# Cross attention with the keys on the partitions, and its softmax run beside the next sequence's projections

## The reference

```python
q = (x @ Wq).reshape(B, N, 8, 64).transpose(0, 2, 1, 3)        # x: layer-normed, N = 128
k = (context @ Wk).reshape(B, M, 8, 64).transpose(0, 2, 1, 3)  # M = 2048
v = (context @ Wv).reshape(B, M, 8, 64).transpose(0, 2, 1, 3)
attn = softmax(einsum('bhnd,bhmd->bhnm', q, k) * scale, axis=-1)
out = einsum('bhnm,bhmd->bhnd', attn, v)
```

## Time and profile before

| | |
|---|---|
| median of 3 runs | 1711.84 us (1708.66 to 1711.86) |
| the profiled execution, own time | 1703.06 us |
| its span, first to last instruction | 1701.1 us |
| PE busy | 1634.1 us (96%) |
| DVE, ACT, POOL busy | 648.4, 663.5, 541.3 us (38%, 39%, 32%) |
| granted clock of PE | 0.99 on average |

### The profile page before, as it was taken

The page is one execution under the profiler, slowest core; times in us unless marked ns, Lnnn a source line. Parts: engine busy times, 40 slices in busy tenths (PEclk is TensorE's granted clock), DMA queues, the critical chain, the costliest instruction groups (busy, mean ns, idle before and its releaser), DMA issues. The chain is left out here.

```text
span 1701.1 us, 23083 instructions
## 1 busy us (share of the span) xinstructions
PE 1634.1 (96%) x9230; PEld 1290.6 (76%) x9231; DVE 648.4 (38%) x1079; ACT 663.5 (39%) x1196; POOL 541.3 (32%) x326
## 2 busy tenths in 40 slices
PE   7999999999999999999999999998889998999998
PEld 6667887887887888788788888773457686877876
DVE  6316325424523523632532542444365461222222
ACT  3225334434433533533433443342444433354421
POOL 6221132044043023124113304003620046768661
PEclk9999999999999999999999999999999998999999
DMA  5230121121111021021012112014200076656521
GB/s 209 88 99 26 39 68 50 32 74 50 32 63 46 17 81 50 26 73 59 25 32 75 50 32 81 1 36 170 75 1 1 21 259 143 172 148 188 162 56 35
DMA packets 70393, 125.15 MB, mean 74 GB/s; under 512 B 12000, under 2 KB 28448, under 8 KB 70304
## 3 DMA queue, kind: packets, MB, share of 16 engines
q1 hardware_dynamic: 40192, 92.14, 16.6%
q10 hardware_dynamic: 25296, 23.34, 4.7%
q0 software_dynamic: 4816, 8.41, 2.6%
HBM read 100.74 MB, written 24.43 MB: 74 GB/s over the span
## 5 line engine op out<-in xcount | busy, mean ns | idle before, releaser
L220 POOL TENSOR_TENSOR ctx_h<-stage,one 128x1024 fp32r<-128x1024 f32 x62 | 117.4, 1894 | 759.1 <-PE ps_t L288 759.1
L288 PE MATMUL ps_s<-ctx_h,wk 128*128 128x512 f32 x1024 | 325.4, 393 | 9.3 <-DVE ctx_l L498 9.3
L288 PE MATMUL ps_t<-wv,ctx_h 128*128 128x512 f32 x1024 | 317.7, 392 | 0.0
L542 DVE TENSOR_TENSOR kT<-ps_s,kT 64x512 fp32r<-64x512 f32 x128 | 87.5, 683 | 426.2 <-ACT kT L455 425.4
L288 PEld LDWEIGHTS ps_s<-ctx_h,wk 128*128 128x128 f32 x1024 | 193.5, 189 | 49.7 <-issue 9.9
L288 PEld LDWEIGHTS ps_t<-wv,ctx_h 128*128 128x128 f32 x1024 | 192.3, 188 | 42.3 <-issue 2.9
L564 DVE TENSOR_REDUCE smax<-ps_s 128x1 f32<-128x1024 f32 x128 | 150.6, 1218 | 142.1 <-PE ps_s L306 140.9
L288 PE MATMUL ps_s<-ctx_l,wk 128*128 128x512 f32 x512 | 200.3, 391 | 0.0
L288 PE MATMUL ps_t<-wv,ctx_l 128*128 128x512 f32 x512 | 199.3, 389 | 0.0
L438 ACT ACTIVATE probs<-ps_s,nmax 128x1024 f32<-128x1024 f32 x128 | 142.0, 1123 | 91.6 <-DVE nmax L567 91.6
L454 ACT ACTIVATE kT<-ps_s 64x512 fp32r<-64x512 f32 x128 | 75.6, 591 | 261.8 <-PE ps_s L288 168.3
(11 more groups left out here) (236 smaller groups left out, 2228.1 us busy)
## 6 DMA issues: line engine op xcount, KB each, us to landing
stage<-in_ctx_dram SPq DMA_DIRECT2D x64, 512.0 KB, 3.8
raw_u<-in_up_dram SPq DMA_DIRECT2D x32, 512.0 KB, 4.0
stage<-in_down_dram SPq DMA_DIRECT2D x16, 512.0 KB, 4.0
raw_e<-in_down_dram SPq DMA_DIRECT2D x16, 512.0 KB, 4.1
rows_scratch<-wxo SPq DMA_DIRECT2D x25, 256.0 KB, 4.6
wxo<-rows_scratch ACTq DMA_DIRECT2D x23, 256.0 KB, 3.4
q_scratch<-kT ACTq DMA_DIRECT2D x4, 1024.0 KB, 5.5
qa<-q_scratch ACTq DMA_DIRECT2D x32, 128.0 KB, 3.0
```

The costliest lines, as they stand in the source:

```text
L220: nc.gpsimd.tensor_tensor(hi, raw, one[:, 0:1].unsqueeze(2).broadcast_to([P, 2, QT]), ALU.mult).then_inc(hi_done, 1)
L288: mm = nc.tensor.matmul(out, w(c), m(c), start=(c + k == 0), stop=(c == DC - 1 and k == 2))
L542: nc.vector.tensor_tensor(kT[XD:P, 0, p, keys], ps_s[0:XD, p, :], kT[0:XD, 0, p, keys], ALU.subtract)
```

## The change

**What it does.** (1) Keys on the partitions: the weights of a score product are now 128 keys of one pair (`kT`, both heads' 64 dimensions on 128 partitions), and the moving side is `q2`, 256 columns: for head 0 its queries on the first 64 partitions and zeros on the others, for head 1 the other way (block diagonal). High and rest are again three products. Per group and pair there are 4 x 3 = 12 matmuls of 256 columns, 192 per sequence. The 128 transposes, their copies and the ACT accumulator go. (2) Scores are made group by group, and ACT copies them to `s` in SBUF (`copy_score`), DVE keeps a running maximum in `top` (`max_scores`), and `kT` holds one group only. (3) The largest score of a latent is now across partitions: PE turns the maxima (`turn_max`), DVE reduces them and puts them on a diagonal (`diagonal`), PE spreads them to all partitions by a product with ones (`spread_max`), DVE subtracts (`shift`, 128x2048 per head), ACT does exp (`exps`), POOL adds up the 16 chunks (`tree`), and PE sums over the partitions (`sums`). DVE takes the reciprocal of a 128x512 tile (`output`). (4) Shift, exp and tree of sequence b-1 run while PE projects sequence b; its `values` stand behind the value projections of b's first group. After the last sequence they have nothing beside them, and half of the row sums are made on PE (`sums_of_chunks`). (5) ACT makes `ctx_h` (`round_ctx`), POOL only the rest. (6) Sequence 0 begins with the values of two groups, and the key exit is one 128-partition instruction each on ACT and DVE.

```diff
-                        keys = kT[:, h % 2, h // 2, j * 512:(j + 1) * 512]
-                        nc.tensor.matmul(ps_s[:, j, :], qa[:, h, :], keys, start=True, stop=False)
-                        mm = nc.tensor.matmul(ps_s[:, j, :], qb[:, h, :], keys, start=False, stop=True)
...
-                        for i in range(4):
-                            mm = nc.tensor.transpose(ps_t[:, n % 3, i, :],
-                                                     probs[:, e, (4 * j + i) * P:(4 * j + i + 1) * P], ident[:, :])
...
+            def scores(b, g, p):
+
+                n = nth_s(b, g, p)
+                pe.wait_ge(k_lo, nth_k(b, g, p) + 1)
+                pe.wait_ge(q_in, (b + 1) * (16 * 4))
+                if n >= 2:
+                    pe.wait_ge(max_done, 2 * (n - 1))
+                for i in range(4):
+                    out = ps_e[:, 2 * (n % 2) + i // 2, i % 2].rearrange("p e t -> p (e t)")
+                    for c, (w, m) in enumerate(((0, 0), (0, 1), (1, 0))):
+                        mm = nc.tensor.matmul(out, kT[:, w, p, i * P:(i + 1) * P],
+                                              q2[:, p, m].rearrange("p e t -> p (e t)"), start=(c == 0), stop=(c == 2))
+                mm.then_inc(s_done, 1)
...
+            for b in range(1, B):
+                for p in range(PAIRS):
+                    project_k(b, 0, p)
+                    if p == 0:
+                        for i in range(1, PAIRS):
+                            turn_max(b - 1, i)
+                    else:
+                        spread_max(b - 1, p)
+                for t in range(4):
+                    project_v(b, 0, t)
+                for p in range(PAIRS):
+                    values(b - 1, p)
+                keys_and_scores(b, 1)
+                values_and_scores(b, 1, lambda t: sums(b - 1, range(XH)) if t == 1 else None)
+                for p in range(PAIRS):
+                    project_k(b, 2, p)
+                values_and_scores(b, 2)
+                last_group(b)
...
+            for b in range(1, B):
+                exps(b - 1, 0)
+                for p in range(3):
+                    key_hi(b, 0, p)
+                exps(b - 1, 1)
+                key_hi(b, 0, 3)
+                for t in range(3):
+                    copy_v(b, 0, t)
+                    exps(b - 1, t + 2)
+                for h in range(5, XH):
+                    exps(b - 1, h)
+                copy_v(b, 0, 3)
+                round_ctx(b, (4, 5))
...
+            def diagonal(b, p):
+
+                dve.wait_ge(t_done, b * PAIRS + p + 1)
+                nc.vector.tensor_reduce(mcol[:, 2 * p:2 * p + 2], max_room(p).rearrange("p (e t) -> p e t", e=2), AX_X,
+                                        ALU.max).then_inc(mcol_done, 1)
+                dve.wait_ge(mcol_done, b * PAIRS + p + 1)
+                if p >= 2:
+                    dve.wait_ge(m_spread, b * PAIRS + p - 1)
+                for e in range(2):
+                    ins = nc.vector.tensor_scalar(diag[:, p % 2, e, :], ident[:, :], mcol[:, 2 * p + e:2 * p + e + 1], None,
+                                                  ALU.mult)
+                ins.then_inc(diag_done, 1)
+
+            def shift(b, h):
+
+                dve.wait_ge(m_spread, b * PAIRS + h // 2 + 1)
+                largest_score = max_room(h // 2)[:, h % 2 * T:(h % 2 + 1) * T].unsqueeze(1).broadcast_to([P, MT, T])
+                nc.vector.tensor_tensor(s[:, h], s[:, h], largest_score, ALU.subtract).then_inc(shifted, 1)
```

More of the change, by code:

```diff
@@ new lines, in sum_place, with sums, sums_of_chunks @@
+            def sum_place(h):
+                return ps_m[h % 2 * XD:(h % 2 + 1) * XD, h // 2 * T:(h // 2 + 1) * T]
+            def sums(b, heads):
+                pe.wait_ge(sum_done, b * XH + len(heads))
+                for h in heads:
+                    mm = nc.tensor.matmul(sum_place(h), ones, sum_room(b, h), start=True, stop=True)
+                mm.then_inc(l_done, 1)
+            def sums_of_chunks(p):
+                for t in range(MT):
+                    for h in (2 * p, 2 * p + 1):
+                        nc.tensor.matmul(sum_place(h), ones, s[:, h, t, :], start=(t == 0), stop=(t == MT - 1))
@@ new lines, in exps, with keys_and_scores @@
+            def exps(b, h):
+                act.wait_ge(shifted, b * XH + h + 1)
+                for j in range(2):
+                    part = s[:, h, 8 * j:8 * j + 8, :]
+                    nc.scalar.activation(part, part, ACT.Exp, scale=X_SCALE).then_inc(exp_done, 1)
+            def keys_and_scores(b, g, also=None):
+                for p in range(PAIRS):
+                    key_hi(b, g, p)
+                    copy_score(b, g - 1, p)
+                    if also:
+                        also(p)
@@ new lines, in _ @@
+            for t in range(4):
+                copy_v(0, 1, t)
+                if t >= 2:
+                    query_hi(t - 2)
+            for p in range(PAIRS):
+                key_hi(0, 0, p)
+                if p < 2:
+                    query_hi(p + 2)
+            round_ctx(0, (4, 5))
+            keys_and_scores(0, 1, lambda p: query_hi(PAIRS + p))
+            round_ctx(0, (6, 7))
+            keys_and_scores(0, 2)
+            values_and_scores(0, 2)
+            round_ctx(1, (0, 1))
@@ L489, in _ @@
+            for h in range(XH):
+                exps(LASTB, h)
         @block.vector
@@ L597, in self_attention @@
+            shift(LASTB, 0)
+            diagonal(LASTB, 1)
+            diagonal(LASTB, 2)
+            shift(LASTB, 1)
+            diagonal(LASTB, 3)
+            for h in range(2, XH):
+                shift(LASTB, h)
+            output(LASTB)
 def self_attention(nc, x_ap, bo_ap, wxo, wxo_in, wq_ap, wkd_ap, wvd_ap, wku_ap, wvu_ap, wo_ap, wg_ap, up_ap, down_ap,
```

713 lines of the change are left out of this document (422 added, 291 removed).

## The result

| | before | after |
|---|---|---|
| median | 1711.85 us (1708.66 to 1715.26, 4 runs) | 1667.35 us (1664.71 to 1667.58, 4 runs) |
| ratio, 95% interval | | 0.9736 (0.9715 to 0.9757) |
| profiled execution, own time | 1703.06 us | 1667.58 us |
| span | 1701.1 us | 1665.7 us |
| end of the cross attention | 1140.51 us | 1095.73 us |

The change makes the kernel 44.5 us faster; 24.5 were forecast. The cross attention alone ends 44.8 us earlier. So the comparison goes by the end of the cross attention.

The account below looks back on a forecast made before the run. PE's work was taken to bound the cross attention. Opening -29, seven periods -32, end +36.5 make -24.5 us: 1678.6 against the profiled 1703.1, 1687 as median; 8-in-10 range 1658 to 1710.

Parts of the forecast that it names:

- The sum of the work: PE per period: projections, score products at 0.118 us, values, small products and sums 126.8 us, plus 0.6 for hand-overs.
- so 4.5 us are lost: Start of each period: PE waits for diagonal 1, then value projections for key rests; 4.5 us per period.
- four of them stand behind four of POOL's: Diagonals 1 and 2 on DVE: each of four instructions waits behind a POOL instruction; diagonals there at 9.6 and 11.7 us.
- The second part of the forecast's loss: PE's value projections wait for key rests 2 and 3, delayed to 16.3 and 19.2 us, and end at 27.4.
- a median well above 0.3 us: Profile sign for DVE's diagonal instructions (L771): median well above 0.3 us, maximum above 1.2.
- The first rival: Diagonals don't meet POOL, or both of one pass together: 3.5 us less per period, 1663 us; chance 0.16.
- The opening: Before the seven periods: sequence 0 leaves its values to period 1, ends at 154.9 us, 29 us earlier.
- The end: Behind the last projection: uncovered softmax, values, sums and a 4.6 us reciprocal take 38.2 us, 36.5 us later than before.
- the clock could be taken as nothing: In the end, PE's clock falls early, where exps are waited for anyway: 0 to 4 us more, taken as 0.
- The trees: Rival: POOL's row sums, forecast 5.3 us per head, come late for the next scores' copies; 1702 us at 6.4; chance 0.12.
- The break-even: POOL's tree time per head at which the whole gain is gone: 6.6 us; beyond it the kernel is slower.
- Weight loads: Rival: loads of 188 ns bound the score products, up to 0.188 us each, 108 us more, 1795 us; chance 0.06.

Follow-up runs that it names:

- run 4: Changed kernel with diagonals 1 and 2 first on DVE, two POOL rests behind the first tree, that tree behind diagonal 2, fourth key tile before exp 1: 1651.48 us.
- run 8: Changed kernel without the third score product (low part of keys times high part of queries), 64 of 192 per sequence: 1603.49 us.
- run 7: Changed kernel with one more POOL addition in each head's tree, in seven of eight sequences: 1716.35 us.
- run 6: Changed kernel reordered so that softmax and values of a sequence finish before the next one's key projections: 1751.93 us.
- run 2: Changed kernel with diagonals 1 and 2 ahead of the first key rest in DVE's queue: 1674.77 us.

## Why the prediction was right, and what it mis-sized

**The bound.** PE's work sets the period (runs 4 and 8). The sum of the work, 126.8 + 0.6, was right to 0.1 us against run 4, out of one price that no row showed: the score product, taken as 0.118, is 0.120 (192 x 0.002 = 0.4 us more), which stands against values of 14.13 in place of 14.6.

**The stall, "so 4.5 us are lost".** This is the step that was mis-sized, 1.97 in place of 4.5, 7 x 2.5 = 18 us. The mechanism was right: contention with POOL and the order in which DVE's queue reaches diagonal 1. The sentence "four of them stand behind four of POOL's" was wrong. It carried over a whole wait per instruction from the earlier trace rows, where two instructions of 0.54 us met POOL. The diagonals take 0.28, and one of four found POOL between two instructions; the first came 0.4 us before a rest ended and lost 0.24. DVE also came to diagonal 1 earlier, at 6.2 and not 6.8. Diagonal 1 was there at 7.9 (forecast 9.6) and diagonal 2 at 9.5 (11.7), PE waited 1.65 us (3.5), the value projections ended at 24.97 (27.4). The second part of the forecast's loss, about 1 us in which value projections wait for the key rests behind the diagonals, never came: the rests were done at 10.1, 13.7 and 16.5 and not at 12.4, 16.3 and 19.2, and PE waits in no second place. The line as a whole shows how rare the waits are; "a median well above 0.3 us" was a miss:

```profile
L771 DVE TENSOR_SCALAR diag<-ident,mcol x64: 274/286/1302, 146.5 to 1066.8; 128x128 fp32r<-128x128 f32 x64
```

The first rival, no contention at all, would have had 23.9; the truth lay between, nearer to it.

**The opening**: 154.32 against 154.9. The waits for the first scores' operands went, as forecast: from 9 us to 154.32 PE is idle for 0.7 us in all.

**The end**: 35.9 against 38.2. The reciprocal:

```profile
L786 DVE RECIPROCAL on<-ps_m 128x512 f32<-128x512 f32 x8 | 26.8, 3349 | 11.4 <-PE ps_m L450 11.4
```

3.35 us, not 4.6: the slope between 4 and 8 columns was too steep for 512. Values and sums of a pair took 3.50 each and not 3.7, and the first sums ended at 24.2, not 24.9. The clock fell to 0.50 here too, and cost nothing: the third pair's values still came 0.08 us too early for their exps. That the clock could be taken as nothing is partly luck, by this margin.

**The three add up**: 7 x 2.55 + 2.3 + 0.6 = 20.8 us, against the 20 by which the medians miss the forecast. All three errors have the same sign, so none hides another; the stall is by far the largest.

**The rivals.** The trees took 5.5 us per head (forecast 5.3) and were done at 52.9 of a period where ACT's copies of the last pair's scores want them at 56.6; run 7 shows the wait at L411 (L409 of the changed kernel) that would follow, and that 6.9 us per head ends the gain. The break-even, forecast at 6.6, is thus near 6.9. That the smaller stall left more gain to lose, and the clock took part of that back, is my account of the difference. Weight loads: 0.120 us per product with loads of 0.191. The rule of the Trainium skill (TensorE: Matmul & The Clock Gate, "The mechanism") that a load overlaps running products only on another group of rows doesn't hold for these full-array products: by it the kernel would have been slower. The same section of the Trainium skill also says that a load that targets the background weight buffer is pulled ahead of running products. That would fit the pace here, but no run shows where a load goes.

## What to carry to other kernels

A softmax costs little where another stage's products cover it, and a change's whole gain can hang on that cover: without it this one turned from 2.6% faster to 2.2% slower, with the same instructions, though up to 4.6 of the 12.25 us that it lost a period were contention that the new order brought along. An experiment that moves work to take away one thing must be read for what else it moved. Before costing a contention as so many waits, look how long the shorter instruction is and what the other engine runs at that moment; a new order is safe only if it doesn't move the instruction under a longer one, and an operand in PSUM can avoid the question. Where PE is the bound, a wait of 4.6 us costs the wait and the slow products behind it, 2.7 us more here.

## What was not expected of the hardware

- A `tensor_scalar` of 128 columns took 0.28 us alone, up to 1.30 beside POOL's additions, and 2.43 under a rest; with its operand in PSUM 0.341 to 0.352 in all 64 cases.
- After 4.6 us and more without products the granted clock was 0.50 for the next 4.5 us and more, and PE's busy time was 2.9 us (run 6) and 2.7 us (run 7) a period longer; after 1.65 us it stayed at 1.00 in all seven periods. After 0.43 and 1.63 us with 0.39 us of work between (run 2) it stayed in six periods and fell in one, which was 1.6 us longer.
- The reciprocal of 128x512 from PSUM took 3.35 us, 4.8 times a `tensor_tensor` of the same size (0.69).
